# Attention inner loop on eight cores: two heads' score matmuls issued as one interleaved block of four, and one exponential over both heads

## The chip, the cores and the metric

The kernel runs as one program on all 8 cores of one Trainium2 chip. The time is the device time in microseconds (us) of the slowest core, from the start to the end of one execution. Several executions are made and the median is compared.

## The reference

One layer computes, for x of shape (2, 4096, 2048), a layer norm, and on its output both an attention with 32 query heads and 8 key/value heads of 64, and a gated feed-forward network of width 8192. The two are added to x:

```python
xn = _layernorm(x, axis=-1)
# attention
Q = (xn @ Wq.T + bq).reshape(b, t, 32, 64).transpose(0, 2, 1, 3)
K = (xn @ Wk.T + bk).reshape(b, t, 8, 64).transpose(0, 2, 1, 3)
V = (xn @ Wv.T + bv).reshape(b, t, 8, 64).transpose(0, 2, 1, 3)
Q, K = _rope(Q, K)
K, V = jnp.repeat(K, 4, axis=1), jnp.repeat(V, 4, axis=1)
w = softmax(einsum('bhqd,bhkd->bhqk', Q, K) / 8)
attn = einsum('bhqk,bhkd->bhqd', w, V) @ Wo.T + bo
# feed-forward
ffn = (silu(xn @ w_gate.T) * (xn @ w_up.T)) @ w_down.T
return x + attn + ffn
```

## The kernel before

**Split over the cores.** Each core owns 1024 query tokens of one of the two batches. It computes K and V for all 4096 tokens of its batch, Q for its own tokens, attention for its own tokens over all keys, and the feed-forward network for its own tokens. Nothing is exchanged between cores.

**Stages.** The first stage (A_tile, eight tiles of 512 tokens) makes the layer norm, K transposed (kt_all), V (v_all, with a column of ones behind each head's 64) and Q transposed (qt_all), all bf16 and all kept in SBUF. The second stage is attention. The third, in two halves of 512 tokens, computes gate, up, down and output projections with streamed weights (L603, L613, L645, L650).

**Attention.** The loop at L417 runs over 16 pairs of query heads (j). The two heads of a pair are called head a and head b here; their queries lie in rows (SBUF partitions) 0 to 63 and 64 to 127 of qt_all, the two matching key heads likewise in kt_all. For each pair, the loop at L495 runs over 32 chunks of 128 keys (c). What is done for one chunk is:

- S_head (L429, matmuls at L438): scores of one head, 128 keys by 1024 queries, as two matmuls of 512 columns. Head a uses rows 0 to 63 of the TensorE array and writes pb[0]; head b uses rows 64 to 127 and writes pb[1]. pb[0] and pb[1] are PSUM tensors of 1024 fp32 columns (two banks) each. S_head of chunk c waits for that head's exponential of chunk c - 1, which frees its PSUM tensor.
- EXP (L447, ScalarE at L453): one exponential of 128x1024 from PSUM to pta (head a) or ptb (head b), bf16, in one of two halves by the parity of c.
- AV (L458): for head a two matmuls (L467) with 128 rows and 65 columns (64 of V and the ones, which give the softmax denominator) into pb[2]. For head b four matmuls: V at L480 (128 rows, 64 columns, at array columns 64 to 127) and ones at L487 (128 rows, one column), twice each, into pb[3].

TensorE works in program order. That order is written out by hand in the loop at L495, and every engine's program is the list of what was emitted for it: scores of head a for chunk c, AV of head a for chunk c - 1, scores of head b for c, AV of head b for c - 1. So the scores of the two heads are apart by the two matmuls of L467, except in the first chunk of a pair, where there is no earlier AV.

At the end of a pair (L508 to L529) VectorE takes two reciprocals of the denominators (L508, L510), copies both results out (L511, L512), TensorE spreads the reciprocals over 64 rows in fp32 (L515, L519), and VectorE multiplies (L524, L527). TensorE has nothing else to do meanwhile. At the start of a pair VectorE clears head b's accumulator (L419, L421).

Of the kernel before, what the change touches and what calls it, by code (L numbers as in the profile page):

```python
# [17 lines left out]
TOK = 1024  # L18
# [6 lines left out]
NKCH = T // 128  # L25
# [15 lines left out]
S_PE, S_VE, S_SC = "s_pe", "s_ve", "s_sc"  # L41
# [53 lines left out]
def build_nc(debug_names=()):  # L95
# [3 lines left out]
    nc = bass.Bass("TRN2", target_bir_lowering=False)  # L99
    es = ExitStack()  # L100
# [34 lines left out]
    ones_f = sb("ones_f", (1, 128), F32)  # L135
# [7 lines left out]
    nk_sb = sb("nk_sb", (1, 64), F32)  # L143
    sc1_sb = sb("sc1_sb", (1, 8), F32)

    pb = [es.enter_context(nc.psum_tensor(f"pb{i}", [128, 1024], F32)) for i in range(4)]

    em = Em()
    K = {}
# [36 lines left out]
    pstat = pb[0][:, 0:512]
    pnorm = pb[0][:, 512:1024]
    pmub = pb[1][:, 0:512]
    prb = pb[1][:, 512:1024]
    pp = [pb[2][:, 0:512], pb[2][:, 512:1024], pb[3][:, 0:512], pb[3][:, 512:1024]]  # L190
# [186 lines left out]
    for tt in range(NTT):  # L377
# [10 lines left out]
    a5 = em.emit("vector", lambda v: v.tensor_scalar_mul(  # L388
        sc1_sb[0:1, 4:5], sc1_sb[0:1, 3:4], -0.125), waits=[a4])
    a6 = em.emit("tensor", lambda t: t.matmul(  # L390
        pb[0][:, 0:1], ones_f[0:1, :], sc1_sb[0:1, 4:5], start=True, stop=True),
        waits=[a5, em.tok(S_VE)], inc=S_PE)
    a7 = em.emit("vector", lambda v: v.tensor_copy(negb_sb[:, :], pb[0][:, 0:1]),
                 waits=[a6])
    K["negb"] = a7
    for nm_, buf in (("d_negb", negb_sb), ("d_kt", kt_all), ("d_qt", qt_all), ("d_v", v_all)):
# [8 lines left out]
    pta = esB.enter_context(nc.sbuf_tensor("pta", [128, 2 * TOK], BF16))  # L405
    ptb = esB.enter_context(nc.sbuf_tensor("ptb", [128, 2 * TOK], BF16))
# [10 lines left out]
    for j in range(NPAIR):  # L417
        p = j // 4
        m1 = em.emit("vector", lambda v: v.memset(pavb[0:1, :], 0.0),  # L419
                     waits=[av_final, prev_evac])  # L420
        bmemset = em.emit("vector", lambda v: v.memset(pavb[64:128, :], 0.0))  # L421
        exp_a = {}
        exp_b = {}
        av_a = {}
        av_b = {}
        s_a = {}
        s_b = {}

        def S_head(c, hh):  # L429
            base = 64 * hh  # L430
            ps = psa if hh == 0 else psb_
            ex = exp_a if hh == 0 else exp_b
            w_s = [a_ready, a_ready_sc, negb_tok, ex.get(c - 1)]
            if j > 0 and c == 0:
                w_s.append(prev_pair_exp[hh])
            last = None
            for h in range(2):
                last = em.emit("tensor", (lambda p, j, c, h, base, ps: lambda t: t.matmul(  # L438
                    ps[:, 512 * h:512 * (h + 1)],
                    kt_all[base:base + 64, 4096 * p + 128 * c:4096 * p + 128 * (c + 1)],  # L440
                    qt_all[base:base + 64, TOK * j + 512 * h:TOK * j + 512 * (h + 1)],
                    start=True, stop=True))(p, j, c, h, base, ps),
                    waits=(w_s if h == 0 else []),
                    inc=(S_PE if h == 1 else None))
            (s_a if hh == 0 else s_b)[c] = last

        def EXP(c, hh):  # L447
            par = c % 2
            ps = psa if hh == 0 else psb_
            pt = pta if hh == 0 else ptb  # L450
            w_e = [(s_a if hh == 0 else s_b)[c], (av_a if hh == 0 else av_b).get(c - 2)]
            (exp_a if hh == 0 else exp_b)[c] = em.emit(
                "scalar", (lambda par, ps, pt: lambda s: s.activation(  # L453
                    pt[:, TOK * par:TOK * (par + 1)], ps[:, :], AF.Exp,
                    bias=negb_sb[:, :], scale=0.125))(par, ps, pt),
                waits=w_e, inc=S_SC)

        def AV(c, hh):  # L458
            par = c % 2
            first, last = (c == 0), (c == NKCH - 1)  # L460
            if hh == 0:
                w_av = [exp_a[c]]
                if first:
                    w_av.append(prev_evac)
                tok = None
                for h in range(2):
                    tok = em.emit("tensor", (lambda c, p, par, h, first, last: lambda t: t.matmul(  # L467
                        pava[0:65, 512 * h:512 * (h + 1)],
                        v_all[:, VST * c + 65 * (2 * p):VST * c + 65 * (2 * p) + 65],
                        pta[:, TOK * par + 512 * h:TOK * par + 512 * (h + 1)],  # L470
                        start=first, stop=last))(c, p, par, h, first, last),
                        waits=(w_av if h == 0 else []), inc=(S_PE if h == 1 else None))
# [78 lines left out]
    pmub2 = pb[0][:, 0:512]
    prb2 = pb[0][:, 512:1024]
    pg = [pb[1][:, 0:512], pb[1][:, 512:1024]]
    pu = [pb[2][:, 0:512], pb[2][:, 512:1024]]
    pres = [pb[3][:, 0:512], pb[3][:, 512:1024]]
# [236 lines left out]
```

How the kernel before makes its waits and increments, by code:

```python
        def body(eng):  # L686
            waited = {}
            for fn, waits, inc in ops:
                for (s, v) in waits:
                    v16 = 16 * v if is_dma_sem(s) else v
                    if waited.get(s, -1) >= v16:
                        continue
                    eng.wait_ge(sems[s], v16)
                    waited[s] = v16
                inst = fn(eng)
                if inc is not None:
                    if inst is None:
                        raise RuntimeError(f"inc op returned None on {eng_name}")
                    inst.then_inc(sems[inc], 16 if is_dma_sem(inc) else 1)
```

## Time and profile before

| | us |
|---|---|
| median of 3 runs | 5816.5 (5789.39 to 5972.33) |
| the profiled execution | 5785.88 |
| its span, slowest core | 5784.3 |
| span of the fastest core | 5768.6 |

The span is the time from the first to the last instruction of a core; 1.6 us of the profiled execution lie outside it. Engines are named PE (TensorE matmul), PEld (TensorE weight load), DVE (VectorE), ACT (ScalarE), POOL (GpSimd) and SP (SyncE). The granted clock is the share of the full TensorE clock of 2.4 GHz that the chip grants: 1.00 is 2.4 GHz and 0.50 is 1.2 GHz. "pb<-qt_all,kt_all" says what an instruction writes and what it reads, with buffer numbers left out.

### The profile page before, as it was taken

Reading aid. Unit: us, or ns where it says so; the run is one execution under the profiler, and the core shown is the slowest. Engines: PE = TensorE matmul, PEld = TensorE weight load, DVE = VectorE, ACT = ScalarE, POOL = GpSimd, SP = SyncE. Lnnn points to the kernel's source line nnn. Section 1 sums busy time; section 2 is a strip of 40 time slices with the busy share of each in tenths; the row PEclk is TensorE's granted clock in tenths of the full one; section 3 lists DMA queues with packets and bytes.
Section 4 is the critical chain, followed back from the end, with each engine's and each line's share of the span. In section 5 each row is a group of like instructions: output and inputs, shape, how many; then the busy total and the mean of one; then the engine's idle time right before and its main releaser. Section 6 shows DMA issues by size and latency. Waiting matters only on the chain.

```text
span 5784.3 us, 37090 instructions; the slowest of 8 cores (5768.6 to 5784.3 us)
## 1 busy us (share of the span) xinstructions
PE 4790.7 (83%) x13728; PEld 1322.0 (23%) x13898; DVE 902.4 (16%) x1009; ACT 1375.2 (24%) x1612; POOL 224.3 (4%) x428
## 2 busy tenths in 40 slices
PE   4655456488898888988889888998599989699999
PEld 1211111111111111111111111111144434244444
DVE  2333433411101111011110111001210000100000
ACT  1011112133343333433334333443200000000000
POOL 0000000000000000000000000000011100011100
PEclk9878667665555555555555555555599999799999
DMA  4423343300000000000000000000299988699987
GB/s 84 69 62 69 87 91 69 86 9 0 0 0 0 0 0 0 0 0 0 0 0 0 0 0 0 0 0 0 55 145 153 152 153 161 132 153 152 152 163 149
DMA packets 95342, 340.12 MB, mean 59 GB/s; under 512 B 10784, under 2 KB 10816, under 8 KB 90688
## 3 DMA queue, kind: packets, MB, share of 16 engines
q0 software_dynamic: 60608, 274.81, 29.3%
q1 hardware_dynamic: 34560, 62.93, 3.8%
q8 instruction: 117, 1.92, 0.1%
q14 instruction: 57, 0.47, 0.0%
HBM read 604.07 MB, written 8.39 MB: 106 GB/s over the span
## 4 chain that ended last, share of the span: by engine, by line
PE 75%; DMA 10%; DVE 10%; issue 2%; ACT 2%; DVEq 0%; POOL 0%; another core or an unknown queue 0%; ACTq 0%; SPq 0%; POOLq 0%
PE pb L438 17%; PE pb L480 10%; PE pb L487 9%; PE pb L467 9%; PE pb L613 7%; PE pb L603 7%; DMA wo_sb<-wo_t 5%; PE pb L293 5%; PE pb L650 5%; DMA xf_sb<-x_t 3%; PE pb L345 2%; DVE rz_sb L508 2%; DVE rz_sb L510 2%; PE pb L645 1%; DMA xf<-x_t 1%
## 5 line engine op out<-in xcount | busy, mean ns | idle before, releaser
L438 PE MATMUL pb<-qt_all,kt_all 64*128 64x512 bf16 x2048 | 1038.3, 617 | 23.5 <-ACT pta L453 22.9
L453 ACT ACTIVATE pta<-pb,negb_sb 128x1024 bf16<-128x1024 f32 x512 | 570.4, 1114 | 1344.9 <-PE pb L438 1344.9
L453 ACT ACTIVATE ptb<-pb,negb_sb 128x1024 bf16<-128x1024 f32 x512 | 570.3, 1114 | 413.3 <-PE pb L438 413.3
L480 PE MATMUL pb<-ptb,v_all 128*64 128x512 bf16 x1024 | 648.7, 633 | 2.0 <-DVE pb L421 0.5
L487 PE MATMUL pb<-ptb,ones_bf 128*1 128x512 bf16 x1024 | 594.8, 581 | 0.0
L603 PE MATMUL pb<-xt,wg_sb 128*128 128x512 bf16 x2008 | 471.0, 382 | 102.1 <-DVE xt L584 82.0
L467 PE MATMUL pb<-pta,v_all 128*65 128x512 bf16 x1024 | 544.1, 634 | 0.0
L508 DVE RECIPROCAL rz_sb<-pb 1x1024 f32<-1x1024 f32 x16 | 104.8, 6552 | 2527.2 <-PE pb L487 2527.2
L613 PE MATMUL pb<-xt,wu_sb 128*128 128x512 bf16 x2006 | 463.0, 381 | 2.8 <-DMA wu_sb<-wu_t 0.4
L650 PE MATMUL pb<-gated,wd_sb 128*128 128x512 bf16 x2009 | 445.2, 379 | 2.1
L293 PE MATMUL pb<-xt_sb,wk_sb 128*128 128x512 bf16 x496 | 194.0, 519 | 214.6 <-DVE xt_sb L274 214.2
L619 ACT ACTIVATE silu_sb<-pb 128x512 bf16<-128x512 f32 x128 | 76.4, 597 | 1186.7 <-PE pb L603 1186.7
L603 PEld LDWEIGHTS pb<-xt,wg_sb 128*128 128x128 bf16 x2048 | 200.5, 98 | 355.0 <-issue 117.2
L480 PEld LDWEIGHTS pb<-ptb,v_all 128*64 128x64 bf16 x1024 | 131.6, 129 | 652.2 <-issue 652.2
L438 PEld LDWEIGHTS pb<-qt_all,kt_all 64*128 64x128 bf16 x2048 | 127.7, 105 | 668.9 <-issue 668.9
L613 PEld LDWEIGHTS pb<-xt,wu_sb 128*128 128x128 bf16 x2048 | 201.3, 98 | 244.8 <-issue 5.6
L650 PEld LDWEIGHTS pb<-gated,wd_sb 128*128 128x128 bf16 x2048 | 200.3, 98 | 241.7
L515 PE MATMUL pb<-rz_sb,ones_f 1*64 1x512 f32 x64 | 58.2, 1062 | 237.8 <-DVE atmp L511 237.8
L622 DVE TENSOR_TENSOR gated<-silu_sb,pb 128x512 bf16<-128x512 bf16 x128 | 88.1, 688 | 796.6 <-PE pb L613 796.6
L467 PEld LDWEIGHTS pb<-pta,v_all 128*65 128x65 bf16 x1024 | 96.2, 145 | 421.8 <-issue 421.8
L487 PEld LDWEIGHTS pb<-ptb,ones_bf 128*1 128x1 bf16 x1024 | 80.9, 79 | 445.7 <-issue 445.7
L645 PE MATMUL pb<-attn_sb,wo_sb 128*128 128x512 bf16 x499 | 129.1, 414 | 63.8 <-DMA wo_sb<-wo_t 62.8
(98 smaller groups left out, 1929.4 us busy)
## 6 DMA issues: line engine op xcount, KB each, us to landing
wg_sb<-wg_t POOLq DMA_DIRECT2D x128, 512.0 KB, 6.3
wu_sb<-wu_t POOLq DMA_DIRECT2D x128, 512.0 KB, 6.3
wd_sb<-wd_t POOLq DMA_DIRECT2D x32, 2048.0 KB, 15.6
xf_sb<-x_t SPq DMA_DIRECT2D x128, 256.0 KB, 2.7
xt_sb<-x_t POOLq DMA_DIRECT2D x32, 512.0 KB, 14.0
wk_sb<-wk_t POOLq DMA_DIRECT2D x32, 512.0 KB, 7.0
wq_sb<-wq_t POOLq DMA_DIRECT2D x32, 512.0 KB, 5.1
wo_sb<-wo_t POOLq DMA_DIRECT2D x32, 512.0 KB, 19.1
```

What stands on the lines that cost most here:

```text
L293: mtk = em.emit("tensor", (lambda ppj, wbuf, dc, xb: lambda t: t.matmul(ppj[:, :], wbuf[:, 128 * dc:128 * (dc + 1)], xt_sb[:, xb + TW * dc ...
L345: mtk = em.emit("tensor", (lambda ppj, dc, sub, xb: lambda t: t.matmul(ppj[:, :], xt_sb[:, xb + TW * dc + 128 * sub: xb + TW * dc + 128 * ...
L438: last = em.emit("tensor", (lambda p, j, c, h, base, ps: lambda t: t.matmul(ps[:, 512 * h:512 * (h + 1)], kt_all[base:base + 64, 4096 * p ...
L453: "scalar", (lambda par, ps, pt: lambda s: s.activation(pt[:, TOK * par:TOK * (par + 1)], ps[:, :], AF.Exp, bias=negb_sb[:, :], scale=0.12 ...
L467: tok = em.emit("tensor", (lambda c, p, par, h, first, last: lambda t: t.matmul(pava[0:65, 512 * h:512 * (h + 1)], v_all[:, VST * c + 65 * ...
L480: em.emit("tensor", (lambda c, p, par, h: lambda t: t.matmul(pavb[64:128, 512 * h:512 * (h + 1)], v_all[:, VST * c + 65 * (2 * p + 1):VST ...
L487: tok = em.emit("tensor", (lambda c, par, h: lambda t: t.matmul(pavb[0:1, 512 * h:512 * (h + 1)], ones_bf[:, 0:1], ptb[:, TOK * par + 512 ...
L508: q1 = em.emit("vector", lambda v: v.reciprocal(rz_sb[0:1, 0:TOK], pava[64:65, :]), waits=[av_a[NKCH - 1], av_final])
L603: mg = em.emit("tensor", (lambda par, dc: lambda t: t.matmul(pg[par][:, :], wg_sb[:, 2048 * par + 128 * dc:2048 * par + 128 * (dc + 1)], x ...
L613: mu_ = em.emit("tensor", (lambda par, dc: lambda t: t.matmul(pu[par][:, :], wu_sb[:, 2048 * par + 128 * dc:2048 * par + 128 * (dc + 1)], ...
L645: mm = em.emit("tensor", (lambda par, cc, th: lambda t: t.matmul(pres[par][:, :], wo_sb[:, 2048 * par + 128 * cc:2048 * par + 128 * (cc + 1)],
L650: mm = em.emit("tensor", (lambda par, hc: lambda t: t.matmul(pres[par][:, :], wd_sb[:, 8192 * par + 128 * hc:8192 * par + 128 * (hc + 1)], ...
```

## The change

The PSUM tensors pb[0] and pb[1] become one tensor pb01 of 2048 columns, at the same place; pta and ptb become one tensor ptab of twice their size. In each chunk, the four score matmuls stand together and alternate between the heads (head a's first 512 columns, head b's first 512, head a's second, head b's second). They wait once, for the exponential of the chunk before. One exponential of 128x2048 does both heads. Then come the AV matmuls of both heads for the chunk before. The array position of each matmul is the same as before (the argument dropped at L485 and L491 is what the position defaults to). The first and third stage only use the new names.

```diff
-        def S_head(c, hh):
-            base = 64 * hh
-            ps = psa if hh == 0 else psb_
-            ex = exp_a if hh == 0 else exp_b
-            w_s = [a_ready, a_ready_sc, negb_tok, ex.get(c - 1)]
+        def S_quad(c):
+            w_s = [a_ready, a_ready_sc, negb_tok, exp_ab.get(c - 1)]
             if j > 0 and c == 0:
-                w_s.append(prev_pair_exp[hh])
+                w_s.append(prev_pair_exp)
             last = None
             for h in range(2):
-                last = em.emit("tensor", (lambda p, j, c, h, base, ps: lambda t: t.matmul(
-                    ps[:, 512 * h:512 * (h + 1)],
+                for hh in range(2):
+                    base = 64 * hh
+                    off = 1024 * hh + 512 * h
+                    last = em.emit("tensor", (lambda p, j, c, h, base, off: lambda t: t.matmul(
+                        pscore[:, off:off + 512],
...
-        def EXP(c, hh):
+        def EXP(c):
             par = c % 2
...
-            w_e = [(s_a if hh == 0 else s_b)[c], (av_a if hh == 0 else av_b).get(c - 2)]
...
+            w_e = [s_ab[c], av_b.get(c - 2)]
+            exp_ab[c] = em.emit("scalar", (lambda par: lambda s: s.activation(
+                ptab[:, 2048 * par:2048 * (par + 1)], pscore[:, :], AF.Exp,
+                bias=negb_sb[:, :], scale=0.125))(par), waits=w_e, inc=S_SC)
...
         for c in range(NKCH):
-            S_head(c, 0)
-            EXP(c, 0)
+            S_quad(c)
+            EXP(c)
             if c >= 1:
                 AV(c - 1, 0)
-            S_head(c, 1)
-            EXP(c, 1)
-            if c >= 1:
                 AV(c - 1, 1)
```

TensorE's program over one chunk, before. L438 writing pb0 are the scores of head a, writing pb1 those of head b; L467 is AV of head a, L480 and L487 are AV of head b; x2 is two instructions in a row.

```order
L438 MATMUL pb0<-qt_all,kt_all 128x512 [waits s_sc]
L438 MATMUL pb0<-qt_all,kt_all 128x512
L467 MATMUL pb2<-pta,v_all 65x512 x2
L438 MATMUL pb1<-qt_all,kt_all 128x512 [waits s_sc]
L438 MATMUL pb1<-qt_all,kt_all 128x512
L480 MATMUL pb3<-ptb,v_all 64x512
L487 MATMUL pb3<-ptb,ones_bf 1x512
L480 MATMUL pb3<-ptb,v_all 64x512
```

The same chunk on TensorE in the changed kernel:

```order
L438 MATMUL pb01<-qt_all,kt_all 128x512 [waits s_sc]
L438 MATMUL pb01<-qt_all,kt_all 128x512 x3
L463 MATMUL pb2<-ptab,v_all 65x512 x2
L476 MATMUL pb3<-ptab,v_all 64x512
L482 MATMUL pb3<-ptab,ones_bf 1x512
L476 MATMUL pb3<-ptab,v_all 64x512
L482 MATMUL pb3<-ptab,ones_bf 1x512
L438 MATMUL pb01<-qt_all,kt_all 128x512 [waits s_sc]
```

Head b's scores have moved ahead of head a's AV, and the chunk has one wait for ScalarE (s_sc) where it had two.

ScalarE's program at the start of attention, before (the casts of L355 are the end of the first stage):

```order
L355 CAST v_all<-pb2 128x64 x7
L386 ACTIVATE sc1_sb<-sc1_sb 1x1 [waits s_ve]
L453 ACTIVATE pta<-pb0,negb_sb 128x1024 [waits s_pe]
L453 ACTIVATE ptb<-pb1,negb_sb 128x1024 [waits s_pe]
L453 ACTIVATE pta<-pb0,negb_sb 128x1024 [waits s_pe]
L453 ACTIVATE ptb<-pb1,negb_sb 128x1024 [waits s_pe]
```

The same in the changed kernel, up to the third stage:

```order
L357 CAST v_all<-pb2 128x64 x7
L388 ACTIVATE sc1_sb<-sc1_sb 1x1 [waits s_ve]
L450 ACTIVATE ptab<-pb01,negb_sb 128x2048 [waits s_pe] x512
L610 ACTIVATE silu_sb<-pb01 128x512 [waits s_pe] x2
L610 ACTIVATE silu_sb<-pb01 128x512 [waits s_pe,s_ve] x126
```

The 1024 exponentials of 1024 columns have become 512 of 2048.

## Rows read from the trace of the kernel before

**Rows 1.** The page: busy time of each engine, and clock in 40 slices
```profile
PE 4790.7 (83%) x13728; PEld 1322.0 (23%) x13898; DVE 902.4 (16%) x1009; ACT 1375.2 (24%) x1612; POOL 224.3 (4%) x428
...
PEclk9878667665555555555555555555599999799999
```

**Rows 2.** Windows: start:end, length, busy per engine (instructions), clock, DMA share, GB/s
```profile
1214.10:4140.00 2925.90, 2660.38 (x5248) 456.36 (x5249) 316.86 (x128) 1140.29 (x1025) 0.00 (x0) 0.50 0.00 0
1410.00:1556.00 146.00, 146.00 (x289) 24.75 (x288) 0.00 (x0) 63.62 (x58) 0.00 (x0) 0.50 0.00 0
4205.00:4645.00 440.00, 434.85 (x1983) 197.59 (x2021) 44.03 (x64) 37.62 (x63) 67.03 (x127) 1.00 1.01 151
```

**Rows 3.** Timeline of one chunk: start, length, engine, line [idle before, released by]
```profile
2502.11 1.06 PE L467 MATMUL pb<-pta,v_all 128*65 128x512 bf16 x2
...
2503.11 1.03 PE L438 MATMUL pb<-qt_all,kt_all 64*128 64x512 bf16 x2
...
2504.07 0.63 PE L480 MATMUL pb<-ptb,v_all 128*64 128x512 bf16 x1
2504.24 1.11 ACT L453 ACTIVATE ptb<-pb,negb_sb 128x1024 bf16<-128x1024 f32 x1 [0.85 <-PE pb L438]
...
2504.64 0.58 PE L487 MATMUL pb<-ptb,ones_bf 128*1 128x512 bf16 x1
...
2506.23 1.03 PE L438 MATMUL pb<-qt_all,kt_all 64*128 64x512 bf16 x2
...
2507.19 1.06 PE L467 MATMUL pb<-pta,v_all 128*65 128x512 bf16 x2
```

**Rows 4.** Timeline at the start of the second pair, and of the third
```profile
1397.82 1.04 PE L438 MATMUL pb<-qt_all,kt_all 64*128 64x512 bf16 x4
...
1398.95 1.11 ACT L453 ACTIVATE pta<-pb,negb_sb 128x1024 bf16<-128x1024 f32 x1 [24.97 <-PE pb L438]
...
1400.21 1.01 PE L438 MATMUL pb<-qt_all,kt_all 64*128 64x512 bf16 x2 [1.35 <-ACT pta L453]
...
1405.42 1.03 PE L438 MATMUL pb<-qt_all,kt_all 64*128 64x512 bf16 x2
...
1580.29 1.04 PE L438 MATMUL pb<-qt_all,kt_all 64*128 64x512 bf16 x4
```

**Rows 5.** Timeline at the first chunk of the first pair
```profile
1214.12 0.61 PE L438 MATMUL pb<-qt_all,kt_all 64*128 64x512 bf16 x4 [0.59 <-DVE negb_sb L393]
```

**Rows 6.** Windows around the start of attention and two ends of a pair, columns as in rows 2
```profile
1212.00:1214.80 2.80, 0.96 (x6) 0.44 (x6) 0.89 (x3) 0.72 (x9) 0.00 (x0) 1.00 0.00 0
1556.30:1559.70 3.40, 3.40 (x8) 0.66 (x7) 0.00 (x0) 0.69 (x1) 0.00 (x0) 0.51 0.00 0
1559.70:1563.10 3.40, 0.85 (x3) 0.19 (x2) 2.38 (x1) 0.00 (x0) 0.00 (x0) 1.00 0.00 0
1924.90:1928.30 3.40, 1.02 (x4) 0.27 (x3) 2.20 (x1) 0.00 (x0) 0.00 (x0) 1.00 0.00 0
```

**Rows 7.** Timeline of TensorE at the end of the second pair
```profile
1554.75 1.03 PE L438 MATMUL pb<-qt_all,kt_all 64*128 64x512 bf16 x2
1555.71 0.63 PE L480 MATMUL pb<-ptb,v_all 128*64 128x512 bf16 x1
...
1559.83 0.41 PE L480 MATMUL pb<-ptb,v_all 128*64 128x512 bf16 x1
...
1560.17 0.38 PE L487 MATMUL pb<-ptb,ones_bf 128*1 128x512 bf16 x1
```

**Rows 8.** ScalarE alone by lines and shapes: count, busy us, mean ns, idle before
```profile
L453 ACT ACTIVATE pta<-pb,negb_sb 128x1024 bf16<-128x1024 f32 x512 | 570.4, 1114 | 1344.9 <-PE pb L438 1344.9
L619 ACT ACTIVATE silu_sb<-pb 128x512 bf16<-128x512 f32 x128 | 76.4, 597 | 1186.7 <-PE pb L603 1186.7
L355 ACT CAST v_all<-pb 128x64 bf16<-128x64 f32 x256 | 33.0, 251 | 142.3 <-PE pb L349 142.3
L298 ACT ACTIVATE scrb<-pb,bk_sb 128x512 bf16<-128x512 f32 x32 | 22.0, 687 | 547.8 <-PE pb L293 547.8
```

More of the change, by code:

```diff
@@ L144, in build_nc @@
     sc1_sb = sb("sc1_sb", (1, 8), F32)
-    pb = [es.enter_context(nc.psum_tensor(f"pb{i}", [128, 1024], F32)) for i in range(4)]
+    pb01 = es.enter_context(nc.psum_tensor("pb01", [128, 2048], F32))
+    pb2 = es.enter_context(nc.psum_tensor("pb2", [128, 1024], F32))
+    pb3 = es.enter_context(nc.psum_tensor("pb3", [128, 1024], F32))
     em = Em()
@@ L184, in build_nc @@
     K["init_ve"] = em.tok(S_VE)
[L186 to L190, printed above, removed]
+    pstat = pb01[:, 0:512]
+    pnorm = pb01[:, 512:1024]
+    pmub = pb01[:, 1024:1536]
+    prb = pb01[:, 1536:2048]
+    pp = [pb2[:, 0:512], pb2[:, 512:1024], pb3[:, 0:512], pb3[:, 512:1024]]
     state = dict(xt_free={}, rope_done=None, last_red=None,
@@ L390, in build_nc @@
     a6 = em.emit("tensor", lambda t: t.matmul(
-        pb[0][:, 0:1], ones_f[0:1, :], sc1_sb[0:1, 4:5], start=True, stop=True),
+        pb01[:, 0:1], ones_f[0:1, :], sc1_sb[0:1, 4:5], start=True, stop=True),
         waits=[a5, em.tok(S_VE)], inc=S_PE)
-    a7 = em.emit("vector", lambda v: v.tensor_copy(negb_sb[:, :], pb[0][:, 0:1]),
+    a7 = em.emit("vector", lambda v: v.tensor_copy(negb_sb[:, :], pb01[:, 0:1]),
                  waits=[a6])
@@ L434, in S_head @@
             if j > 0 and c == 0:
-                w_s.append(prev_pair_exp[hh])
+                w_s.append(prev_pair_exp)
             last = None
             for h in range(2):
-                last = em.emit("tensor", (lambda p, j, c, h, base, ps: lambda t: t.matmul(
-                    ps[:, 512 * h:512 * (h + 1)],
[L440 to L444, printed above, removed]
@@ L445, in S_head @@
-            (s_a if hh == 0 else s_b)[c] = last
-        def EXP(c, hh):
-            par = c % 2
-            ps = psa if hh == 0 else psb_
-            pt = pta if hh == 0 else ptb
-            w_e = [(s_a if hh == 0 else s_b)[c], (av_a if hh == 0 else av_b).get(c - 2)]
[L452 to L456, printed above, removed]
+                for hh in range(2):
[3 more added lines that the diff above has]
+                        pscore[:, off:off + 512],
+                        kt_all[base:base + 64, 4096 * p + 128 * c:4096 * p + 128 * (c + 1)],
+                        qt_all[base:base + 64, TOK * j + 512 * h:TOK * j + 512 * (h + 1)],
+                        start=True, stop=True))(p, j, c, h, base, off),
+                        waits=(w_s if (h == 0 and hh == 0) else []),
+                        inc=(S_PE if (h == 1 and hh == 1) else None))
@@ L458, in AV @@
+            s_ab[c] = last
+        def EXP(c):
+            par = c % 2
+            w_e = [s_ab[c], av_b.get(c - 2)]
+            exp_ab[c] = em.emit("scalar", (lambda par: lambda s: s.activation(
+                ptab[:, 2048 * par:2048 * (par + 1)], pscore[:, :], AF.Exp,
+                bias=negb_sb[:, :], scale=0.125))(par), waits=w_e, inc=S_SC)
         def AV(c, hh):
@@ L461, in AV @@
             if hh == 0:
-                w_av = [exp_a[c]]
+                w_av = [exp_ab[c]]
                 if first:
@@ L474, in AV @@
             else:
-                w_av = [exp_b[c]]
+                w_av = [exp_ab[c]]
                 if first:
@@ L482, in AV @@
                         v_all[:, VST * c + 65 * (2 * p + 1):VST * c + 65 * (2 * p + 1) + 64],
-                        ptb[:, TOK * par + 512 * h:TOK * par + 512 * (h + 1)],
-                        start=False, stop=False, skip_group_check=True,
-                        tile_position=(0, 64)))(c, p, par, h),
+                        ptab[:, 2048 * par + 1024 + 512 * h:2048 * par + 1024 + 512 * (h + 1)],
+                        start=False, stop=False, skip_group_check=True))(c, p, par, h),
                         waits=(w_av if h == 0 else []))
@@ L488, in AV @@
                         pavb[0:1, 512 * h:512 * (h + 1)], ones_bf[:, 0:1],
-                        ptb[:, TOK * par + 512 * h:TOK * par + 512 * (h + 1)],
-                        start=False, stop=False, skip_group_check=True,
-                        tile_position=(0, 0)))(c, par, h),
+                        ptab[:, 2048 * par + 1024 + 512 * h:2048 * par + 1024 + 512 * (h + 1)],
+                        start=False, stop=False, skip_group_check=True))(c, par, h),
                         inc=(S_PE if h == 1 else None))
@@ L549, in build_nc @@
     out_sb = sbC("out_sb", (128, 2 * TW), F32)
[L551 to L555, printed above, removed]
+    pmub2 = pb01[:, 0:512]
+    prb2 = pb01[:, 512:1024]
+    pg = [pb01[:, 1024:1536], pb01[:, 1536:2048]]
+    pu = [pb2[:, 0:512], pb2[:, 512:1024]]
+    pres = [pb3[:, 0:512], pb3[:, 512:1024]]
     attn_done = K["attn_done"]
```

16 lines of the change are left out of this document (7 added, 9 removed).

## Prediction, made before the changed kernel was run

> **What bounds the kernel now.** I read the page first, for how the engines' busy shares and the TensorE clock lie over the span [rows 1]. PE is busy 83% of it, and the clock digits fall to 5 in the middle half of the span. The windows by stage put a number on that: attention is 2926 us, half of the span, PE is busy in it for 2660 us, and the mean granted clock is 0.50 (1.2 GHz). The gate and up projections run at 1.00 (2.4 GHz) [rows 2]. No DMA moves in attention. Inside a pair of heads PE has no gap at all: 146.00 of 146 us, with ScalarE busy for 63.6 us of these [rows 2]. So TensorE sets the time of attention, at half its clock.
>
> The timeline gives the price of each block of matmuls, from start to start [rows 3]. Head a's AV takes 2503.11 - 2502.11 = 1.00 us, one head's scores 4.07 - 3.11 = 0.96, head b's AV 6.23 - 4.07 = 2.16. A chunk is 0.96 + 1.00 + 0.96 + 2.16 = 5.08 us for 10 matmuls; the two L467 blocks shown are 5.08 apart. At 1.2 GHz the 512 columns of a matmul are 0.427 us, so about 0.08 us of each is not streaming.
>
> From pair to pair 182.47 us pass (1397.82 to 1580.29) [rows 4]. I cut this into four parts. The start, to the scores of the third chunk: 1405.42 - 1397.82 = 7.60. Then 29 chunks of 5.08 = 147.3, to the scores of the last chunk. Then the tail, up to the last matmul start at 1560.17 [rows 7]: 7.4. Then 20.1 in which VectorE makes the reciprocals and the result is scaled.
>
> **The change, part by part.**
>
> Scores side by side. The two heads use different rows of the array (0 to 63, and 64 to 127). Apart, each pair of matmuls costs 0.96 us. At a pair's start, where no AV stands between them, all four took 1.04 us from the first start to the last end [rows 4]; one head's two alone take 1.03 [rows 3]. So the heads' matmuls run at the same time, and the block of four costs what two did: 0.96 us from start to start. The order is new within the block (a, b, a, b instead of a, a, b, b). From below it can't be under 0.96, since each head still has two matmuls in its own rows. From above it is four matmuls one after another, each at the dearest spacing in the rows, 0.57 (L480 to L487 [rows 3]): 2.27. I take 0.96, because rows 4 show the same four instructions. At half clock a chunk becomes 0.96 + 1.00 + 2.16 = 4.12 us. AV is the same work in the same array positions.
>
> One exponential. No row shows 2048 columns. On ScalarE [rows 8], L298 (512 columns, with a bias tile) takes 687 ns, L453 (1024, with a bias tile) 1114: 427 ns for 512 more columns. That gives 1114 + 854 = 1968 ns. From above it is two of the present ones, 2228. From below, the slope from L355 (64 columns, 251) to L619 (512, 597) is 0.772 ns a column, which gives 1905. I take 1.97 us, since it rests on the two rows with the same kind of operands. The exponentials save little time on ScalarE, which has room at half clock.
>
> One wait where there were two. The scores of a chunk now wait for the whole exponential of the chunk before, and the exponential waits for all four matmuls. Queued behind the waiting scores is the AV of the chunk before, which is already allowed to run but can't pass. The loop is: from the exponential's end to the first matmul 0.15 (1398.95 + 1.11 = 1400.06, to 1400.21), four matmuls 1.04 at half clock, hand-over 0.09 (1397.82 + 1.04 = 1398.86, to 1398.95) [rows 4], exponential 1.97. That is 3.25 us, under the 4.12 that TensorE needs. At half clock AV (3.16 us) covers the exponential, and the saving is TensorE's own 0.96 us a chunk.
>
> The start of a pair stays as it is. Scores at 0, exponential from 1.13 to 3.10, scores of chunk 1 at 3.25, AV of chunk 0 at 4.2, its head b at 5.2, scores of chunk 2 at 7.4 to 7.6. Now it is 7.60. The pair's end is untouched.
>
> The clock. This is the larger term, and no page row prices it. In the steady part PE is busy without a gap and still has 0.50 [rows 2]. At the end of the second pair the engine does AV alone from 1555.71 on, matmuls that use all 128 rows, and no scores. In that stretch (1556.3 to 1559.7) the clock is still 0.51, and in the next it is 1.00 [rows 6]; L480 and L487 take 0.41 and 0.38 us there [rows 7] where they took 0.63 and 0.58 [rows 3]. It is the same at the fourth pair's end (1924.9). PE is as busy before as in the steady part. What differs is that the steady part has four matmuls in ten that fill half of the rows. The changed loop has no such stretch: when scores run, both halves of the rows work. So I expect the clock to rise soon after a pair's start. At full clock 512 columns are 0.213 us. The AV block is six matmuls, 3.16 - 6 x 0.213 = 1.88 us. The four scores took 0.61 us from first start to last end at the only place where they ran at 1.00 [rows 5, 6], and their block costs 0.96 - 2 x 0.213 = 0.53. TensorE needs 0.53 + 1.88 = 2.41 us a chunk. The loop of scores and exponential needs 0.15 + 0.61 + 0.09 + 1.97 = 2.82 us, and now it is the longer one: PE waits 0.4 us a chunk, far less than at a pair's end. I take 2.82. It has bounds 2.76 and 3.08 from those of the exponential.
>
> On which of the two loops binds, the Trainium skill has a rule against hoping for TensorE's own time (TensorEngine Tiling (Array Packing), section PSUM Bottleneck): tiling speeds up TensorE but not the reading of PSUM, which may become the bottleneck. The rows agree. By TensorE alone the time would come out 0.41 x 28 x 16 = 184 us lower than the sum below, at 4526.
>
> **Sum.** A pair: start 7.60; one chunk still at half clock, 4.12; 28 at 2.82 = 79.0; tail to the last matmul start 2.82 + 1.88 - 0.30 = 4.4; end 20.1. Together 115.2, against 182.47: 67.2 saved, times 16 = 1076. From the profiled execution, 5785.88, that leaves 4710 us. That execution lies 0.5% under the median of the runs shown (5816.5), close to the lowest, so I leave the sum as it is.
>
> **Rivals.**
>
> 1. The clock stays at 0.50 in the steady part. For it: PE is already busy all the time at 0.50, and the change doesn't make it busier; nothing in the trace shows four interleaved scores in a dense stretch. Against it: the rise after AV alone. A pair is then 7.6 + 29 x 4.12 + (4.12 + 3.16 - 0.5) + 20.1 = 154.0, 28.5 saved, 456 in all: 5330 us. The Trainium skill bears on this (TensorE: Matmul & The Clock Gate, Part 1): the default state is throttled and activity releases the throttle. Taken as plain busy time, the trace disagrees: 146.00 us of 146 busy at 0.50. By that reading the change could not touch the clock, and this rival would be the forecast.
>
> 2. The clock swings. At full clock PE has a wait in each chunk, so it may fall, rise and fall again. Halfway between 2.82 and 4.12 is 3.47 a chunk: 0.65 x 28 x 16 = 291 us more than the forecast, 5001. Against it: at 2.82 us a chunk the same columns pass in less time than at 4.12.
>
> 3. Slower. The alternating order drains the array at each change of rows, so that the heads don't run together. With 0.57 us a matmul the block is 2.27, a chunk 2.27 + 3.16 = 5.43 at 0.50 clock, 0.35 x 29 x 16 = 162 us more: 5948. It is slower than now once the block costs over 1.92 us. For it: a change of array position costs 0.57 instead of about 0.43 (L467's two start that far apart by 1.00 - 0.57). Against it: [rows 4], where both halves overlap.
>
> 4. No overlap but no drain either: the block costs the present 1.92, a chunk 5.08, and nothing changes: 5786.
>
> **How the numbers follow.** Forecast (clock up, loop bound by scores and exponential) 0.80; rival 1 0.11; rival 2 0.04; rival 3 0.03; rival 4 0.02. The forecast's own range is 4640 to 4850: below, the 1905 ns exponential gives 0.06 x 29 x 16 = 28 less, and hand-overs and an earlier rise of the clock some more; above, the 2228 ns one gives 0.26 x 29 x 16 = 121 more, and a rise two chunks later 2 x 1.3 x 16 = 42. The range given goes from 4620 to 5340, to take in rivals 1 and 2, since the clock term alone is 620 us and was read from a few short stretches. About 2% is what a measurement of this kernel can tell from no change. Faster by more: 0.95 (forecast, rivals 1 and 2); within 2%: 0.02; slower: 0.03.
>
> **What would show it.** In the changed profile: a granted clock near 1.00 in attention; L438's four with 0.61 us from first start to last end; one exponential of 1.97 us; the chain through attention alternating between ScalarE and L438, with PE idle before L438 by some 0.4 us, released by ScalarE; chunks 2.8 us apart; attention some 1850 us long. The prediction is wrong if the clock column stays at 0.50 (then chunks 4.1 us apart with no gap on PE), or if L438 starts more than 0.5 us apart in a block. The first and third stage must keep their lengths.

## The result, and the profile after

The changed kernel takes 4700.53 us (median of 10 runs, 4689.0 to 4920.22), against 5863.35 (10 runs, 5785.92 to 6077.38) for the kernel before measured beside it. The ratio to the kernel before is 0.8104, with a 95% interval of 0.8085 to 0.8122. In some executions of every kernel here one die or both ran at a lower clock for part of the time, which widens the medians; the ratios leave these executions out. Where an experiment has no ratio I compare spans of core 0 with the 5784.3 us of the kernel before.

The page of the changed kernel, the rows that answer to [rows 1], and the parts of its chain of waits by engine and by line:

```profile
span 4699.8 us, 35554 instructions; the slowest of 8 cores (4672.9 to 4699.8 us)
...
PE 3507.9 (75%) x13728; PEld 1225.9 (26%) x13898; DVE 902.1 (19%) x1009; ACT 1244.3 (26%) x1100; POOL 224.4 (5%) x428
...
PEclk9878766666988888888888888879999997999999
...
PE 46%; ACT 22%; DVE 13%; DMA 12%; issue 5%; DVEq 0%; POOL 0%; ACTq 0%; another core or an unknown queue 0%; SPq 0%; POOLq 0%
ACT ptab L450 20%; PE pb L604 9%; PE pb L594 9%; DMA wo_sb<-wo_t 6%; PE pb L438 6%; PE pb L295 6%; PE pb L641 6%; DMA xf_sb<-x_t 3%; PE pb L347 3%; DVE rz_sb L499 2%; DVE rz_sb L501 2%; PE pb L636 2%; DMA xf<-x_t 1%; DVE xt_sb L276 1%; DVE scrf L273 1%
```

TensorE executes the same 13728 matmuls, but is busy 1283 us less: that is not work taken away, it is the same columns at a higher clock and side by side. The clock digits in attention are 8 where they were 5. The exponential is now the largest line of the chain, with 20%.

The windows of the changed kernel (columns as in rows 2): attention, a stretch soon after its start, the dense part of a pair, and the third stage.

```profile
1222.50:3050.00 1827.50, 1366.19 (x5249) 357.44 (x5250) 316.84 (x128) 1008.39 (x513) 0.00 (x0) 0.89 0.00 0
1226.00:1230.00 4.00, 3.36 (x9) 0.69 (x9) 0.00 (x0) 2.46 (x2) 0.00 (x0) 0.50 0.00 0
1230.00:1318.00 88.00, 75.64 (x308) 20.27 (x307) 0.92 (x1) 59.01 (x30) 0.00 (x0) 1.00 0.00 1
...
3050.00:4699.00 1649.00, 1473.84 (x6530) 657.93 (x6664) 156.00 (x224) 77.70 (x129) 170.08 (x322) 0.95 0.88 151
```

Attention went from 2925.9 us (1214.1 to 4140.0) to 1827.3 (1222.5 to 3049.8), that is 1098.6 less. The first stage is 8.4 us longer and the third 5.7 (1650.0 against 1644.3), on another core, with core spans 27 us apart in this execution. Together that is the whole difference of the spans, 1084.5 us. Within attention the clock is 1.00 in the dense part of a pair. It is 0.50 in the first chunks of attention, and from each pair's end, where VectorE makes its reciprocals, until some chunks into the next pair.

One chunk in the dense part, from the timeline of the changed kernel. It answers to [rows 3]:

```profile
1951.21 0.61 PE L438 MATMUL pb<-qt_all,kt_all 64*128 64x512 bf16 x4 [0.38 <-ACT ptab L450]
...
1951.75 0.62 PE L463 MATMUL pb<-ptab,v_all 128*65 128x512 bf16 x2
1951.92 1.97 ACT L450 ACTIVATE ptab<-pb,negb_sb 128x2048 bf16<-128x2048 f32 x1 [0.85 <-PE pb L438]
...
1952.30 0.40 PE L476 MATMUL pb<-ptab,v_all 128*64 128x512 bf16 x1
...
1952.63 0.38 PE L482 MATMUL pb<-ptab,ones_bf 128*1 128x512 bf16 x1
...
1952.94 0.40 PE L476 MATMUL pb<-ptab,v_all 128*64 128x512 bf16 x1
...
1953.28 0.38 PE L482 MATMUL pb<-ptab,ones_bf 128*1 128x512 bf16 x1
...
1954.03 0.61 PE L438 MATMUL pb<-qt_all,kt_all 64*128 64x512 bf16 x4 [0.38 <-ACT ptab L450]
```

From one block of scores to the next are 1954.03 - 1951.21 = 2.82 us. The brackets give both sides of the loop: TensorE sits idle for 0.38 us until the exponential ends, and ScalarE sits idle for 0.85 us until the scores end. Neither engine is full. They take turns on one set of PSUM columns (TensorE also does AV while the exponential runs, but is done with it first).

The start of the second pair in the changed kernel, which answers to [rows 4]:

```profile
1336.65 1.04 PE L438 MATMUL pb<-qt_all,kt_all 64*128 64x512 bf16 x4
...
1339.89 1.04 PE L438 MATMUL pb<-qt_all,kt_all 64*128 64x512 bf16 x4 [2.21 <-ACT ptab L450]
...
1344.23 1.04 PE L438 MATMUL pb<-qt_all,kt_all 64*128 64x512 bf16 x4
1345.20 1.07 PE L463 MATMUL pb<-ptab,v_all 128*65 128x512 bf16 x2
...
1346.19 0.40 PE L476 MATMUL pb<-ptab,v_all 128*64 128x512 bf16 x1
...
1347.48 0.61 PE L438 MATMUL pb<-qt_all,kt_all 64*128 64x512 bf16 x4
```

The third block of scores starts 7.58 us after the first, and within that third chunk the matmuls shorten from 0.63 to 0.40 us: the clock is up 9.5 us after the pair's start.

### The profile page after: what moved, and what is told of

It reads as the page before. It is cut to its first block, busy times and chain, and to the rows that moved or that the text cites. A ratio compares the mean times of both kernels' runs of the same rounds, so it can differ in the third digit from the quotient of the medians.

```text
span 4699.8 us, 35554 instructions; the slowest of 8 cores (4672.9 to 4699.8 us)
## 1 busy us (share of the span) xinstructions
PE 3507.9 (75%) x13728; PEld 1225.9 (26%) x13898; DVE 902.1 (19%) x1009; ACT 1244.3 (26%) x1100; POOL 224.4 (5%) x428
## 3 DMA queue, kind: packets, MB, share of 16 engines
q8 instruction: 115, 1.88, 0.2%
## 4 chain that ended last, share of the span: by engine, by line
PE 46%; ACT 22%; DVE 13%; DMA 12%; issue 5%; DVEq 0%; POOL 0%; ACTq 0%; another core or an unknown queue 0%; SPq 0%; POOLq 0%
ACT ptab L450 20%; PE pb L604 9%; PE pb L594 9%; DMA wo_sb<-wo_t 6%; PE pb L438 6%; PE pb L295 6%; PE pb L641 6%; DMA xf_sb<-x_t 3%; PE pb L347 3%; DVE rz_sb L499 2%; DVE rz_sb L501 2%; PE pb L636 2%; DMA xf<-x_t 1%; DVE xt_sb L276 1%; DVE scrf L273 1%
## 5 line engine op out<-in xcount | busy, mean ns | idle before, releaser
L450 ACT ACTIVATE ptab<-pb,negb_sb 128x2048 bf16<-128x2048 f32 x512 | 1007.1, 1967 | 793.2 <-PE pb L438 793.2
L438 PE MATMUL pb<-qt_all,kt_all 64*128 64x512 bf16 x2048 | 327.4, 395 | 212.1 <-ACT ptab L450 211.3
L476 PE MATMUL pb<-ptab,v_all 128*64 128x512 bf16 x1024 | 420.2, 410 | 3.1 <-DVE pb L423 3.1
L482 PE MATMUL pb<-ptab,ones_bf 128*1 128x512 bf16 x1024 | 391.8, 383 | 0.0
L463 PE MATMUL pb<-ptab,v_all 128*65 128x512 bf16 x1024 | 326.4, 401 | 6.0 <-ACT ptab L450 6.0
L476 PEld LDWEIGHTS pb<-ptab,v_all 128*64 128x64 bf16 x1024 | 110.3, 108 | 341.3 <-issue 341.3
L438 PEld LDWEIGHTS pb<-qt_all,kt_all 64*128 64x128 bf16 x2048 | 72.7, 94 | 380.5 <-issue 380.5
L300 ACT ACTIVATE scrb<-pb,bk_sb 128x512 bf16<-128x512 f32 x32 | 22.0, 687 | 557.5 <-PE pb L295 557.5
L295 PE MATMUL pb<-xt_sb,wq_sb 128*128 128x512 bf16 x501 | 154.7, 474 | 1.2 <-issue 0.8
L295 PEld LDWEIGHTS pb<-xt_sb,wk_sb 128*128 128x128 bf16 x512 | 60.1, 121 | 364.0 <-issue 350.2
```

Source lines behind the costliest of these rows:

```text
L295: mtk = em.emit("tensor", (lambda ppj, wbuf, dc, xb: lambda t: t.matmul(ppj[:, :], wbuf[:, 128 * dc:128 * (dc + 1)], xt_sb[:, xb + TW * dc ...
L438: last = em.emit("tensor", (lambda p, j, c, h, base, off: lambda t: t.matmul(pscore[:, off:off + 512], kt_all[base:base + 64, 4096 * p + 1 ...
L450: exp_ab[c] = em.emit("scalar", (lambda par: lambda s: s.activation(ptab[:, 2048 * par:2048 * (par + 1)], pscore[:, :], AF.Exp, bias=negb_ ...
L476: em.emit("tensor", (lambda c, p, par, h: lambda t: t.matmul(pavb[64:128, 512 * h:512 * (h + 1)], v_all[:, VST * c + 65 * (2 * p + 1):VST ...
```

## The experiments

Three things changed at once: the heads' scores overlap, they stand in one block (so AV does too), and the exponential is one. The clock moved as well. The experiments take these apart. Each starts from the changed kernel, except e5 which starts from the kernel before.

### e1: two exponentials instead of one

```diff
-            exp_ab[c] = em.emit("scalar", (lambda par: lambda s: s.activation(
-                ptab[:, 2048 * par:2048 * (par + 1)], pscore[:, :], AF.Exp,
+            for hh in range(2):
+                exp_ab[c] = em.emit("scalar", (lambda par, hh: lambda s: s.activation(
+                    ptab[:, 2048 * par + 1024 * hh:2048 * par + 1024 * (hh + 1)],
+                    pscore[:, 1024 * hh:1024 * (hh + 1)], AF.Exp,
```

> The changed kernel with its one exponential of 128x2048 cut into two of 128x1024, one per head, both behind the four scores. Theory (the gain is the heads' scores running together and filling all rows, and with that the clock): the clock stays near 0.89 in attention as in the changed kernel; the second exponential starts 1.01 us behind the first (rows 4), so the two end 2.12 us after the start and a chunk is 2.82 + 0.16 = 2.98 us, 28 x 16 x 0.16 = 72 us more: about 4772. Rival (the merged exponential is what lets the clock rise): clock 0.50, chunk 4.12, about 5330.

Measured: ratio to the kernel before 0.8224 (0.8185 to 0.8264), the two lowest executions 4753.57 and 4758.02 us, clock 0.90 in attention. In the timeline of e1 a chunk is 1602.60 - 1599.63 = 2.97 us:

```profile
1599.63 0.61 PE L438 MATMUL pb<-qt_all,kt_all 64*128 64x512 bf16 x4 [0.53 <-ACT ptab L451]
...
1600.34 2.12 ACT L451 ACTIVATE ptab<-pb,negb_sb 128x1024 bf16<-128x1024 f32 x2 [0.85 <-PE pb L438]
...
1602.60 0.61 PE L438 MATMUL pb<-qt_all,kt_all 64*128 64x512 bf16 x4 [0.53 <-ACT ptab L451]
```

The two take 2.12 us where the one takes 1.97, and that 0.15 us goes in full into TensorE's wait (0.53 instead of 0.38). Merging the exponentials is worth about 0.15 x 29 x 16 = 70 us, as the two ratios say too (0.8224 against 0.8104), and has nothing to do with the clock.

### e2: one exponential, but scores apart

```diff
-            S_quad(c)
-            EXP(c)
+            S_head(c, 0)
             if c >= 1:
                 AV(c - 1, 0)
+            S_head(c, 1)
+            EXP(c)
+            if c >= 1:
                 AV(c - 1, 1)
```

> The changed kernel with the merged exponential kept, but head b's scores behind head a's AV again. Theory: the heads' scores no longer run together, the clock stays at 0.50, and the loop through the exponential is 0.15 + 0.96 + 1.00 + 1.04 + 0.09 + 1.97 = 5.21 us a chunk against TensorE's own 5.08: about 5786 + 62 = 5850. Rival (one large exponential a chunk is what raises the clock): clock near 0.9, chunk 3.8 us, about 5210.

Measured: core 0 spans 5823.5 us, 39 more than before. The lowest of five executions is 5849.04. Against the kernel before measured beside it (core 0 at 5753.3 to 5771.4 in its four shortest executions) it is some 60 more, as expected. The clock is 0.51 in attention. From the timeline of e2, two exponentials 1504.56 - 1499.39 = 5.17 us apart, with both blocks of scores between them:

```profile
1499.39 1.97 ACT L450 ACTIVATE ptab<-pb,negb_sb 128x2048 bf16<-128x2048 f32 x1 [3.21 <-PE pb L438]
...
1501.50 1.01 PE L438 MATMUL pb<-qt_all,kt_all 64*128 64x512 bf16 x2
...
1503.43 1.03 PE L438 MATMUL pb<-qt_all,kt_all 64*128 64x512 bf16 x2
...
1504.56 1.97 ACT L450 ACTIVATE ptab<-pb,negb_sb 128x2048 bf16<-128x2048 f32 x1 [3.21 <-PE pb L438]
```

By the chunk, the merged exponential alone is a small loss, since it puts a wait into a TensorE that had none (5.17 against 5.08 a chunk).

### e3: order a, a, b, b

```diff
-            for h in range(2):
-                for hh in range(2):
+            for hh in range(2):
+                for h in range(2):
```

> The changed kernel with the four scores in the order a, a, b, b instead of a, b, a, b. Theory: they overlap in both orders, as at a pair's start in the kernel before, so nothing changes: 4700 within 0.5%, block 0.61 us from first start to last end. Rival (alternation is needed for the overlap): block of four one after another, rows half filled, clock 0.50, chunk 5.08: about 5786.

Measured: ratio 0.8111 (0.8064 to 0.8158), chunk 2.82 us. Alternating is not needed; standing together is enough, as the pair's start of the kernel before had shown.

### e4: head b's scores from the same rows

```diff
-                    base = 64 * hh
+                    base = 0
```

> The changed kernel with head b's scores taken from rows 0 to 63 as head a's are, so head b's own scores are left out. Same order, waits and instruction counts. Theory: the four can't overlap and fill half of the rows, so the block is 1.92 us at 1.2 GHz, the clock stays at 0.50, and a chunk is 5.08 us (the loop through the exponential, 0.15 + 1.9 + 0.09 + 1.97 = 4.1, is hidden): 5786 within 1%. Rival (the clock rises by the new order of scores, AV and waits, whatever rows are filled): clock near 0.9, chunk 0.15 + 1.04 + 0.09 + 1.97 = 3.25, about 4910.

Measured: core 0 spans 4971.9 us, clock 0.86 in attention. Here my theory missed, and the rival's 3.25 us a chunk is nearly what the trace has (3.23). The timeline of e4 near the start of a pair (its first scores, not shown, start at 1597.57), TensorE only:

```profile
1606.61 1.88 PE L438 MATMUL pb<-qt_all,kt_all 64*128 64x512 bf16 x4
1608.42 1.06 PE L463 MATMUL pb<-ptab,v_all 128*65 128x512 bf16 x2
...
1611.06 0.58 PE L482 MATMUL pb<-ptab,ones_bf 128*1 128x512 bf16 x1
1611.58 1.29 PE L438 MATMUL pb<-qt_all,kt_all 64*128 64x512 bf16 x4
...
1615.07 1.02 PE L438 MATMUL pb<-qt_all,kt_all 64*128 64x512 bf16 x4 [0.38 <-ACT ptab L450]
...
1618.30 1.02 PE L438 MATMUL pb<-qt_all,kt_all 64*128 64x512 bf16 x4 [0.38 <-ACT ptab L450]
```

The windows of e4 around that place:

```profile
1601.70:1608.40 6.70, 6.70 (x14) 1.39 (x14) 0.91 (x1) 1.97 (x1) 0.00 (x0) 0.50 0.01 2
1608.40:1612.00 3.60, 3.60 (x9) 0.75 (x9) 0.00 (x0) 1.97 (x1) 0.00 (x0) 0.50 0.00 0
1612.20:1660.00 47.80, 42.45 (x149) 12.15 (x147) 0.00 (x0) 29.37 (x15) 0.00 (x0) 1.00 0.00 0
```

The scores don't overlap (1.88 us for four, 1.02 at the full clock). The block of six AV matmuls, the second of this pair, runs from 1608.42 to 1611.58, and the clock is at 1.00 right behind it. I had overlooked that the change also makes AV one block. The kernel before had such a stretch of AV only at a pair's end, and its clock rose there too [rows 6]. So bunching looks like a second way to the same clock, but e4 can't tell it from rival theories. That called for e7.

This second way is not dependable. Within the same core of e4, later pairs (the first line, from the pair that starts at 2382.27) kept 0.50 through seven such blocks of AV, and the clock rose only 38.7 us after the pair's start, against 14.6 us in the pair above. Of the 15 pairs behind the first, 5 rose late. The kernel before is no steadier: AV stands alone in the same way at each of its 16 pair ends, and the clock rose at 8 of them, every second one. The second line is the end of its third pair:

```profile
2415.00:2420.00 5.00, 5.00 (x11) 1.03 (x10) 0.00 (x0) 2.00 (x2) 0.00 (x0) 0.50 0.00 0
1742.20:1743.70 1.50, 1.36 (x3) 0.21 (x2) 0.00 (x0) 0.00 (x0) 0.00 (x0) 0.50 0.00 0
```

### e5: the kernel before, with scores over all rows

```diff
-                    kt_all[base:base + 64, 4096 * p + 128 * c:4096 * p + 128 * (c + 1)],
-                    qt_all[base:base + 64, TOK * j + 512 * h:TOK * j + 512 * (h + 1)],
+                    kt_all[:, 4096 * p + 128 * c:4096 * p + 128 * (c + 1)],
+                    qt_all[:, TOK * j + 512 * h:TOK * j + 512 * (h + 1)],
```

> The kernel before, unchanged in order, waits and counts, but each score matmul reads all 128 rows of K and Q (so it sums both heads' products, and the per-head scores are left out). TensorE is no busier than before. Theory (the clock follows how many rows the running matmuls fill): it rises in attention to about 0.9 with no other change; TensorE's chunk is 5.08 - 10 x 0.213 = 2.95 us, a pair saves about 29 x 2.1 us less some half-clock chunks: about 4820. Rival (the clock follows TensorE's busy time or how the waits lie): clock 0.50, 5786, no change.

Measured: core 0 spans 4587.7 us; clock 0.90 in attention. In a dense stretch of e5 TensorE is as fully busy as before (55.00 of 55 us), but at clock 1.00:

```profile
1545.00:1600.00 55.00, 55.00 (x205) 18.50 (x204) 0.00 (x0) 43.67 (x42) 0.00 (x0) 1.00 0.00 1
```

Nothing of the order, the waits or the busy share was touched, and 1197 us went. This excludes plain busy time as what the clock follows, and shows that filling the rows is enough by itself. I had expected about 4820, so the size was missed: the chunk is 2.68 us, not 2.95, which is 0.27 x 29 x 16 = 125 us of the difference. The rest, some 100 us, I didn't take apart. The timeline of e5 shows where the chunk is shorter:

```profile
1559.85 0.60 PE L438 MATMUL pb<-qt_all,kt_all 128*128 128x512 bf16 x2
1560.29 0.59 PE L467 MATMUL pb<-pta,v_all 128*65 128x512 bf16 x2
1560.72 0.59 PE L438 MATMUL pb<-qt_all,kt_all 128*128 128x512 bf16 x2
1561.25 0.40 PE L480 MATMUL pb<-ptb,v_all 128*64 128x512 bf16 x1
...
1562.53 0.61 PE L438 MATMUL pb<-qt_all,kt_all 128*128 128x512 bf16 x2
```

Two scores before head a's AV cost 0.44 us, and that AV before scores 0.43, which is hardly more than two times 0.213. Two scores before L480, which sits at another array position, cost 0.53. I had counted 0.53, 0.57 and 0.53.

### e6: the chunk cut by query columns

```diff
-            S_quad(c)
-            EXP(c)
+            S_pair(c, 0)
+            EXP(c, 0)
             if c >= 1:
                 AV(c - 1, 0)
+            S_pair(c, 1)
+            EXP(c, 1)
+            if c >= 1:
                 AV(c - 1, 1)
```

S_pair is both heads' scores for one half of the queries, side by side in rows, into its own 1024 PSUM columns; EXP(c, h) reads those and waits for them alone.

> The changed kernel with the chunk cut by query columns: scores of both heads for queries 0 to 511, an exponential of 128x1024 over them, AV of head a for the chunk before, scores of both heads for queries 512 to 1023, a second exponential, AV of head b. Each half has its own wait. Theory (the changed kernel is bound by the loop of scores and exponential, TensorE needs only 2.41): the loop no longer binds; TensorE needs 2 x 0.32 + 0.57 + 1.31 = 2.52 us a chunk with clock still near 0.9, 0.30 x 28 x 16 = 134 less: about 4566. Rival (TensorE's real need is near 2.8, or the two exponentials a chunk cost what the overlap gains): 4700 to 4780.

Measured: ratio 0.7887 (0.7843 to 0.793), the lowest execution 4547.54 us, chunk 1552.02 - 1549.54 = 2.48 us (2.52 expected). In a dense stretch of e6 TensorE has next to no idle time left. The window and the two scores that begin a chunk:

```profile
1542.00:1600.00 58.00, 57.84 (x235) 16.47 (x234) 0.00 (x0) 49.23 (x48) 0.00 (x0) 1.00 0.00 1
...
1549.54 0.39 PE L438 MATMUL pb<-qt_all,kt_all 64*128 64x512 bf16 x2
...
1552.02 0.39 PE L438 MATMUL pb<-qt_all,kt_all 64*128 64x512 bf16 x2
```

So the changed kernel was bound by the loop of scores and exponential, not by TensorE, and two exponentials cost nothing visible once they run beside the other half's work.

### e7: e6 with head b's scores from the same rows

The edit is that of e4, made to e6.

> The kernel of e6 with head b's scores taken from rows 0 to 63 too, so head b's own scores are left out; order, waits and counts as in e6, where the clock rose. e4 had shown the clock rising without any overlap, where the six AV matmuls, which fill all rows, stand in one block of 3.2 us. Here AV is cut by scores as in the kernel before. Theory (the clock follows the rows that the matmuls of a stretch fill; in e4 a stretch of AV alone did it): clock 0.50, chunk 5.08 us, 5786 within 1%. Rival (the new order, the waits or two exponentials by query halves raise the clock whatever rows are filled): clock near 0.9, chunk 2.9 to 3.0, about 4800.

Measured: ratio to the kernel before 0.9999 (0.9982 to 1.0016). The windows of e7, a dense stretch and attention:

```profile
1410.00:1550.00 140.00, 140.00 (x277) 23.70 (x276) 0.00 (x0) 61.27 (x55) 0.00 (x0) 0.50 0.00 0
1230.00:2900.00 1670.00, 1530.38 (x3004) 264.03 (x3003) 178.23 (x72) 651.81 (x586) 0.00 (x0) 0.50 0.00 0
```

e6 and e7 differ in one number, which rows of the array head b's scores use. One has a clock of 1.00 in the dense part, the other 0.50, and the difference is 0.7887 against 0.9999. The time holds both effects, since the scores of e7 can't overlap either; the clock column holds one. This is the cleanest pair of the study.

### e8: AV over half of the rows

```diff
-                        v_all[:, VST * c + 65 * (2 * p):VST * c + 65 * (2 * p) + 65],
-                        ptab[:, 2048 * par + 512 * h:2048 * par + 512 * (h + 1)],
+                        v_all[0:64, VST * c + 65 * (2 * p):VST * c + 65 * (2 * p) + 65],
+                        ptab[0:64, 2048 * par + 512 * h:2048 * par + 512 * (h + 1)],
```

and the same for L476 and L482.

> The changed kernel with every AV matmul reading only the first 64 of the 128 keys of a chunk, so half of the keys are left out of AV. Order, waits and counts as in the changed kernel. Theory: AV now fills half of the rows, so the clock stays at 0.50 although the scores overlap, and a chunk takes TensorE's 4.12 us at half clock (3.7 if AV's first matmul runs beside head b's last scores): about 5330 (5145). It would measure the gain of the overlap without the clock. Rival (bunching the scores is enough for the clock): clock near 0.9, chunk 2.82, 4700.

Measured: 5271.59 us in the lower of two executions, core 0 spans 5257.0, clock 0.50 in attention. So the rival fell: four scores in one block, overlapping, and six AV matmuls in one block leave the clock down when AV fills half of the rows. Here every score and AV matmul has 64 rows, and e6 mixes 64 and 128 rows at a clock of 1.00, so it is not the mix of the two that holds the clock down. The timeline of e8:

```profile
1980.51 1.04 PE L438 MATMUL pb<-qt_all,kt_all 64*128 64x512 bf16 x4
1981.34 1.06 PE L463 MATMUL pb<-ptab,v_all 64*65 64x512 bf16 x2
...
1984.47 1.03 PE L438 MATMUL pb<-qt_all,kt_all 64*128 64x512 bf16 x4
```

The chunk is 1984.47 - 1980.51 = 3.96 us, between the two that I had given (4.12 and 3.7): AV follows the scores after 0.83 us instead of 0.96. With that 0.13 us put back (0.13 x 29 x 16 = 60 us) the overlap alone, at half clock, comes to about 5332, which is rival 1's 5330.

### e9: e6 with head b's AV grouped

```diff
                         waits=(w_av if h == 0 else []))
+                for h in range(2):
                     tok = em.emit("tensor", (lambda c, par, h: lambda t: t.matmul(
```

> The kernel of e6 with head b's AV in the order V, V, ones, ones instead of V, ones, V, ones. Theory (e6 is bound by TensorE, and each change of array position costs about 0.12 us beyond the 0.213 us of columns): two changes fewer, 2.48 - 0.2 = 2.27 us a chunk, 29 x 16 x 0.2 = 95 us under e6: about 4455. Rival (the exponentials, 2 x 1.01 us, with their hand-overs already bind, or the spacing doesn't depend on the position): no change from e6, 4548.

Measured: ratio 0.7748 (0.7724 to 0.7773), lowest execution 4480.92 us. The chunks alternate between 2.28 and 2.40 us, 2.34 on average. The timeline of e9:

```profile
1960.53 0.39 PE L438 MATMUL pb<-qt_all,kt_all 64*128 64x512 bf16 x2
...
1960.85 0.62 PE L477 MATMUL pb<-ptab,v_all 128*64 128x512 bf16 x2
...
1961.40 0.59 PE L484 MATMUL pb<-ptab,ones_bf 128*1 128x512 bf16 x2
...
1961.92 0.39 PE L438 MATMUL pb<-qt_all,kt_all 64*128 64x512 bf16 x2
```

Head b's AV takes 1961.92 - 1960.85 = 1.07 us, where e6 took 1.28 (1550.74 to 1552.02). The full 0.2 us shows in every other chunk; the other chunks are 0.12 longer. I expected 4455 and got 26 us more. The 0.12 us is a wait for ScalarE: in a long chunk of e9 the scores start at 1547.55, the exponentials of the chunk before end at 1547.89, and head a's AV, which reads them, starts 0.14 us later at 1548.03. Without a wait it starts 0.32 us behind the scores, as in e6. So e9 is at the limit of its exponentials (ScalarE is busy 58 of 65 us), and the rival named here was right in part. This is the fastest version of the study and beats both kernels.

## Why the prediction was right

The forecast was 4710 us, the profiled execution took 4701.35 and the median was 4700.53. Step by step:

- **Scores side by side.** Forecast 0.96 us a block at half clock and 0.53 at full. The trace has 1345.20 - 1344.23 = 0.97 and 1951.75 - 1951.21 = 0.54. e3 confirms that the order within the block doesn't matter, e8 that the overlap is worth what rival 1 gave.
- **The exponential.** Forecast 1968 ns from L298 and L453. The page of the changed kernel has 1967:

```profile
L450 ACT ACTIVATE ptab<-pb,negb_sb 128x2048 bf16<-128x2048 f32 x512 | 1007.1, 1967 | 793.2 <-PE pb L438 793.2
```

- **The loop.** Forecast 0.15 + 0.61 + 0.09 + 1.97 = 2.82, measured 2.82. TensorE was to wait 0.4 us a chunk; it waits 0.38. e6 shows that TensorE could do a chunk in 2.48, and that the loop, not TensorE, set 2.82. By TensorE alone the forecast would have been 4526. The Trainium skill (TensorEngine Tiling (Array Packing), section PSUM Bottleneck) says that tiling doesn't speed up the reading of PSUM, which may become the bottleneck. The trace agrees in part: TensorE waits 0.38 us a chunk for the exponential that reads PSUM, but ScalarE waits 0.85 us too, and e6 reads as many PSUM columns in 2.48 us a chunk. What bound was the turn-taking on one set of columns, not the reading by itself.
- **The start and the rise of the clock.** 7.60 forecast, 7.58 measured. I gave a third chunk all at half clock (4.12); it took 3.25, since the clock rose inside it. A pair is 113.95 us on average (first exponential of the first pair at 1224.53, of the last at 2933.71, over 15) against 115.2, some 20 us over 16 pairs, 14 of them from this third chunk. The first and third stage gave 14 us back the other way.
- **The clock.** Forecast 1.00 after the first chunks, and that is what came. The reason that I gave, how many rows the running matmuls fill, stands by e5 (rows filled, nothing else changed, clock up) and by e6 against e7 (rows half filled, nothing else changed, clock down). It was incomplete: e4 shows that without any overlap the clock still rises, most likely because the six AV matmuls now stand together, though late in 5 of 15 pairs. In the changed kernel both are there. So the prediction's sentence that "what differs is that the steady part has four matmuls in ten that fill half of the rows" is right about the kernel before, but not all of the change's path to the clock runs through the overlap. The sign that the prediction read it from was also weaker than it took it for. It looked at the second and the fourth pair's end, where the clock rose under AV alone; at the first and the third, and at every odd one behind them, the same matmuls ran and the clock stayed at 0.50. The reading held up by e5, e7 and e8, not by those rows; that the forecast rested on two favourable ends was in part luck.

How the gain divides depends on the order in which it is counted. I count attention alone, on core 0, from its first score matmul to its last VectorE result: 2925.7 us before and 1830.4 in the changed kernel. With the overlap first, at half clock, it is 2925.7 - (2397.1 + 60) = 469 us (e8, with its head start put back), and the clock adds 627. With bunching and the clock first, it is 2925.7 - 2105.7 = 820 us (e4), and the overlap adds 275. The merged exponential's 70 us lie in the second share of the first count, since TensorE sets the 3.96 us of e8. In the second count they should lie in the first share, since e4 waits for its one exponential in each chunk; no run shows that one.

Of the rivals, the first (clock stays) and the fourth fell by the clock and the chunk of the changed kernel; the second (the clock swings) fell because in the dense part the clock holds at 1.00 over 88 us, though TensorE waits in each chunk; the third fell by the block of 0.97.

## What to carry to other kernels

A TensorE that is busy without a gap may still run at half its clock; read the granted clock of the dense part, not only the busy share. Matmuls that fill half of the rows cost twice: they waste half of the array, and scattered between full ones they can hold the clock down, so put two of them next to each other in different rows. Gathering the full ones in one block also helped here, but less surely (e4). When a trace shows a clock rising at one place, look at every place with the same work before you rest a forecast on it. When the clock has doubled, look at once for the next loop of waits: here one set of score columns shared by TensorE and ScalarE, and cutting it in two halves, each with both heads' scores for half of the queries, gave 0.7887 against 0.8104.

## What was not expected of the hardware

- The clock rose in e4 with scores that fill half of the rows and don't overlap, right behind a second block of 3.16 us of AV; in another pair it rose only after seven such blocks at 0.50. With the same matmuls scattered (e7) its mean over attention was 0.50, and 0.51 in e2, where head b's scores have their own rows.
- In the kernel before, the same matmuls at the end of a pair ended at 1.00 in every second pair and at 0.50 in the others.
- Two score matmuls over all 128 rows, next to head a's AV, cost 0.44 us at full clock (e5), where four over half of the rows cost 0.54: so the change from 64 rows to 128 seems to cost about 0.1 us. Between matmuls of 128 rows that start at the same array position no such cost shows.
- A 64-row AV matmul started 0.13 us earlier behind 64-row scores (e8, 0.83 against 0.96 us). It reads rows 0 to 63 and the last scores before it use rows 64 to 127, so it may run beside them in part. I didn't test this further.
